# A decoder layer on one core: routing chain beside the shared expert, residual add split between ScalarE and GpSimd

## The chip, the cores and the metric

The kernel runs on one core of one Trainium2 chip, written in Bass, with every wait and semaphore by hand. The metric is the device time of one execution in microseconds (us), median of several. A core has TensorE (PE; its weight loads are shown as PEld), VectorE (DVE), ScalarE (ACT), GpSimd (POOL) and SyncE (SP, which here only starts DMAs). Each engine runs its own queue in order. All data are float32; "fp32r" is the rounded type that PE takes at one column a cycle.

## The reference

One pre-layernorm decoder layer over x of shape (8, 256, 512), that is 2048 tokens or 16 tiles of 128:

```
x = x + attn(layernorm(x))                        # linear attention, 16 heads
x = x + conv(ctx, ctx, layernorm(x), kernel, D)   # long convolution, 32 heads of 8 channels
x = x + ffn(layernorm(x))
ffn: scores = sigmoid(h @ gate_weight.T)          # 16 experts in 4 groups
     keep the 2 groups with the largest sum of their top 2, then the top 4 experts
     w = 2.5 * score / sum of the 4 scores
     out = sum_e w_e * (silu(h @ g_e.T) * (h @ u_e.T)) @ d_e.T      # I = 256
     shared = (silu(h @ sg.T) * (h @ su.T)) @ sd.T                  # every token
```

## The kernel before

It has five stages, each a block with its own SBUF; at a block's end the engines meet.

1. Attention, 0 to about 260 us, and the convolution, to 444. The convolution leaves its result, transposed (channels on partitions), in the tile `QY`.
2. The shared stage, lines 724 to 996, one step per tile of 128 tokens (16 of them). ScalarE copies the tile from `QY` to `ysl`; PE transposes it (`t3`); VectorE adds it from PSUM to `X` (`x2`, line 868) and takes mean and variance; GpSimd makes the reciprocal root (`rstd3`, 811 and 813); VectorE normalizes (`norm`, 878); PE transposes the result (`t4`); ScalarE and VectorE split it into a high part and a low part (`x_hi`, `x_lo`). PE then does gate and up of the shared expert (12 matmuls of 512 columns: a product of split operands takes three, lines 178 to 180), the router (8 of 32 columns), down of the tile before (6 of 512 columns) and a transpose of the hidden layer. VectorE adds the result to `X`, SP stores normalized rows to `xs_d` and `X` to `out`. The steps of neighbouring tiles are interleaved by hand.
3. The routing stage, lines 998 to 1284. VectorE alone runs some 110 dependent small operations over all 16 tiles: top groups, top 4, weights `W4`, counts per expert (two matmuls on PE), position of each token's row in a list sorted by expert and padded to slots of 512 (`DEST`). Then the list is inverted: for each tile VectorE makes one-hots (`colone`, `lowhot`), GpSimd and ScalarE make the products with token number and weight, and PE adds 4 matmuls a tile up into `PS[:, 2]` (`place`). From there come `IDX` (token of each row) and `WPOS` (its weight).
4. The slots, lines 1287 to 1535. 19 slots here, each of 512 rows of one expert. GpSimd gathers the rows by four indirect DMAs (`gathers`), PE transposes them, ScalarE and VectorE split them and the expert's weights, PE does gate and up with weights stationary (48 matmuls of 512 columns), and down of the slot before (24). ScalarE scales by `WPOS`, GpSimd adds to `out` by four indirect DMAs (`scatters`).

The order in each engine's queue is written out by hand in the `body` and `step` functions.

Of the kernel before, what the change touches and what calls it, by code (L numbers as in the profile page):

```python
# [16 lines left out]
P = 128  # L17
# [26 lines left out]
def decoder_program(nc, x, ctx2, qwT, kwT, vwT, owT, q_b, k_b, v_b, o_b, ssm, dskip, gateT, ebias,  # L44
                    gu_w, dn_w, c_ident, c_block, c_head, c_lt4, c_tri, c_free, c_slotk,
                    c_tok, out):
    with ExitStack() as ctx:
# [5 lines left out]


        kpad_d = nc.dram_tensor("kpad_d", (CH, KPAD + 1), F32).ap()
        xs_d = nc.dram_tensor("xs_d", (B * S + SLOT, D), F32).ap()
# [8 lines left out]
        Tz = [sb(f"Tz{k}", [P, D]) for k in range(2)]  # L65
        C2 = [sb(f"C2{k}", [P, DC * B, 2 * CD]) for k in range(2)]
# [7 lines left out]
        QY = sb("QY", [P, DC, B, S])  # L74
# [494 lines left out]
        zrow = sb("zrow", [P, D])  # L569
# [26 lines left out]
        with nc.Block() as block_:  # L596
            @block_.sync
            def _(sp):
# [5 lines left out]
                for t in range(SLOT_T):  # L604
                    rows = slice(B * S + t * P, B * S + (t + 1) * P)
                    sp.dma_start(xs_d[rows], zrow[:]).then_inc(zero_out, 16)
                    sp.dma_start(out[rows], zrow[:]).then_inc(zero_out, 16)
# [116 lines left out]
        x3h = [sb(f"x3h{p}", [P, DC, P], F32R) for p in range(2)]  # L724
        x3l = [sb(f"x3l{p}", [P, DC, P], F32R) for p in range(2)]
        sg = [sb(f"sg{p}", [P, I_FF]) for p in range(2)]
        hh = [sb(f"hh{p}", [P, I_FF]) for p in range(2)]
        hTh = [sb(f"hTh{p}", [P, IC, P], F32R) for p in range(2)]
        hTl = [sb(f"hTl{p}", [P, IC, P], F32R) for p in range(2)]
        LG = sb("LG", [P, NT, NE])  # L730
        table_row = sb("table_row", [P, 1])

# [6 lines left out]
        r_in = sem("r_in")  # L739
        st3 = ExitStack()  # L740

        def sb3(name, shape, dt=F32):
            return st3.enter_context(nc.sbuf_tensor(name, shape, dt))
        ysl = [sb3(f"ysl{p}", [P, DC, P]) for p in range(2)]
        xn3 = [sb3(f"xn3{p}", [P, D]) for p in range(2)]
        bst3 = [sb3(f"bn_stat3{p}", [P, 6]) for p in range(2)]
        mv3 = [sb3(f"mean_var3{p}", [P, 2]) for p in range(2)]
        ve3 = [sb3(f"var_eps3{p}", [P, 1]) for p in range(2)]
        rs3 = [sb3(f"rstd3{p}", [P, 1]) for p in range(2)]

        def pair(name):
            return [sem(f"{name}{p}") for p in range(2)]
        ysl_done, t3_ps, x2_done, bn3, mv3s, ve3s, rs3s, xn3_done = (
            pair(n) for n in ("ysl_done", "t3_ps", "x2_done", "ln2_bn", "ln2_mv", "ln2_ve", "ln2_rstd", "ln2_xn"))
        xs_out, t4_ps, x3_hi, x3_lo, rt_ps, lg_done, gu_ps, silu_done, h_done = (
            pair(n) for n in ("xs_out", "t4_ps", "x3_hi", "x3_lo", "rt_ps", "lg_done", "gu_ps", "silu_done", "h_done"))
        t5_ps, h_hi, h_lo, dn_ps, x3_done = (pair(n) for n in ("t5_ps", "h_hi", "h_lo", "dn_ps", "x3_done"))
        x3_out = sem("x3_out")


        def bank_chunks(bank, c=DC):
            return PS[:, bank, 0:c * P].rearrange("p (c n) -> p c n", c=c)

        def both_parts(bank):
            return PS[:, bank].rearrange("p (c n i) -> p c n i", c=IC, n=2)

        def gate_up(pe, p, done):
            for d in range(DC):
                mm = three_pass(pe, PS[:, 3 + p].rearrange("p (c n) -> p c n", c=IC), x3h[p][:, d], x3l[p][:, d],
                                gu_row(wh, d), gu_row(wl, d), d == 0, d == DC - 1)  # L770
            mm.then_inc(done, 1)

        def down(pe, p, done):
            for c in range(IC):
                mm = three_pass(pe, PS[:, 6 + p], hTh[p][:, c], hTl[p][:, c], wh[:, DC + c], wl[:, DC + c],
                                c == 0, c == IC - 1)
            mm.then_inc(done, 1)

        with nc.Block() as block_:
            @block_.sync  # L780
            def _(sp):

                sp.dma_start(eb[:], bass.AP(tensor=ebias.tensor, offset=0, ap=[[0, P], [1, NE]])).then_inc(r_in, 16)
                for dst, src in ((lt4, c_lt4), (tri, c_tri), (free, c_free), (slotk, c_slotk), (tok, c_tok)):
                    sp.dma_start(dst[:], src).then_inc(r_in, 16)

                def store_xn(i, p):
                    sp.wait_ge(xn3_done[p], i + 1)
                    sp.dma_start(xs_d[bass.ds((TPB * i + p) * P, P)], xn3[p][:]).then_inc(xs_out[p], 16)

                def store_x(i, p):

                    sp.wait_ge(x3_done[p], i + 1)
                    sp.dma_start(out[bass.ds((TPB * i + p) * P, P)], X[:, TPB * i + p]).then_inc(x3_out, 16)

                store_xn(0, 0)
                store_xn(0, 1)
                with sp.Fori(0, B - 1) as i:
                    for p in range(2):
                        store_xn(i + 1, p)  # L800
                        store_x(i, p)
                store_x(B - 1, 0)
                store_x(B - 1, 1)
                for p in range(2):
                    sp.wait_ge(xs_out[p], 16 * B)

            @block_.gpsimd
            def _(pool):
                def rstd3(i, p):
                    wait_apart(pool, mv3s[p], i + 1)  # L810
                    nc.gpsimd.tensor_scalar(ve3[p][:], mv3[p][:, 1:2], LN_EPS, None, ALU.add).then_inc(ve3s[p], 1)
                    pool.wait_ge(ve3s[p], i + 1)
                    nc.gpsimd.tensor_tensor(rs3[p][:], ve3[p][:], nhalf[:, 0:1], ALU.pow).then_inc(rs3s[p], 1)

                with pool.Fori(0, B) as i:
                    for p in range(2):
                        rstd3(i, p)

            @block_.scalar
            def _(act):  # L820
                def stage_y(i, p, first=False):

                    if not first:
                        wait_apart(act, t3_ps[p], i)
                    act.activation(ysl[p][:], QY[:, :, i, p * P:(p + 1) * P], ACT.Copy).then_inc(ysl_done[p], 1)

                def x_hi(i, p):
                    act.wait_ge(t4_ps[p], i + 1)
                    act.activation(x3h[p][:], bank_chunks(1), ACT.Copy).then_inc(x3_hi[p], 1)

                def silu(i, p):
                    act.wait_ge(gu_ps[p], i + 1)
                    act.activation(sg[p][:].rearrange("p (c n) -> p c n", c=IC), both_parts(3 + p)[:, :, 0], ACT.Silu
                                   ).then_inc(silu_done[p], 1)

                def hid_hi(i, p):
                    act.wait_ge(t5_ps[p], i + 1)
                    act.activation(hTh[p][:], bank_chunks(5, IC), ACT.Copy).then_inc(h_hi[p], 1)

                def step(i, p, last=False):  # L840

                    if not last or p == 0:
                        x_hi(i + p, 1 - p)
# [747 lines left out]
```

## Time and profile before

| | |
|---|---|
| median of 3 runs | 1023.42 us (1021.2 to 1024.94) |
| the profiled execution | 1022.06 us |
| its span, first to last instruction | 1020.2 us |
| mean granted clock of TensorE | 0.942 |
| busy: PE, DVE, ACT, POOL | 88%, 60%, 38%, 38% |

The span is one execution under the profiler. Stages can be told by their lines: 443.9 is the first copy of the shared stage (L825), 556 the sigmoid of the routing stage (L1084), 586.3 the first placement matmul (L1118), 621.9 the first step of the slots.

### The profile page before, as it was taken

Reading aid. Unit: us, or ns where it says so; the run is one execution under the profiler, and the core shown is the slowest. Engines: PE = TensorE matmul, PEld = TensorE weight load, DVE = VectorE, ACT = ScalarE, POOL = GpSimd, SP = SyncE. Lnnn points to the kernel's source line nnn. Section 1 sums busy time; section 2 is a strip of 40 time slices with the busy share of each in tenths; the row PEclk is TensorE's granted clock in tenths of the full one; section 3 lists DMA queues with packets and bytes.
Section 4 is the critical chain, followed back from the end, with each engine's and each line's share of the span. In section 5 each row is a group of like instructions: output and inputs, shape, how many; then the busy total and the mean of one; then the engine's idle time right before and its main releaser. Section 6 shows DMA issues by size and latency. Waiting matters only on the chain. (4 is left out here: it accounts for less than half of the span.)

```text
span 1020.2 us, 14917 instructions
## 1 busy us (share of the span) xinstructions
PE 897.3 (88%) x4428; PEld 739.2 (72%) x4428; DVE 614.0 (60%) x944; ACT 384.0 (38%) x658; POOL 391.8 (38%) x349
## 2 busy tenths in 40 slices
PE   4899999997779999949997095999999999999963
PEld 4788888885567777738885074778878878788752
DVE  5566666655269999966674993454454454454520
ACT  4322323331133343323232053455555555555521
POOL 3200000001156566711110053466666766766622
PEclk9999999998889999959999587999999999999987
DMA  8200000000333333202221011587887887878824
GB/s 318 95 1 1 0 0 0 0 1 0 132 125 104 108 109 110 74 27 74 82 82 72 0 63 62 168 185 203 196 197 194 193 207 194 183 202 205 184 43 60
DMA packets 47272, 108.54 MB, mean 106 GB/s; under 512 B 6736, under 2 KB 7248, under 8 KB 47120
## 3 DMA queue, kind: packets, MB, share of 16 engines
q0 software_dynamic: 17024, 39.86, 20.4%
q1 hardware_dynamic: 30224, 68.38, 20.3%
q8 instruction: 13, 0.21, 0.1%
q14 instruction: 11, 0.09, 0.0%
HBM read 77.73 MB, written 30.49 MB: 106 GB/s over the span
## 5 line engine op out<-in xcount | busy, mean ns | idle before, releaser
L189 PE MATMUL PS<-prod,Tz 128*128 128x288 f32 x640 | 161.7, 417 | 9.4 <-POOL prod L174 9.4
L1342 POOL DMA_INDIRECT out_y<-yo,idy x76 | 139.4, 1834 | 58.5 <-ACT yo L1386 46.3
L189 PEld LDWEIGHTS PS<-prod,Tz 128*128 128x128 f32 x640 | 125.1, 196 | 45.6 <-issue 6.0
L178 PE MATMUL PS<-xTh,wh 128*128 128x512 f32 x304 | 126.6, 416 | 7.7 <-issue 7.7
L180 PE MATMUL PS<-xTh,wl 128*128 128x512 f32 x304 | 120.4, 396 | 0.0
L179 PE MATMUL PS<-xTl,wh 128*128 128x512 f32 x304 | 120.0, 395 | 0.0
L1331 POOL DMA_INDIRECT xg<-xs_d,idx x76 | 86.5, 1138 | 35.4 <-issue 17.5
L1444 DVE TENSOR_TENSOR hTl<-hh,hTh 128x512 fp32r<-128x512 f32 x38 | 26.5, 697 | 111.9 <-ACT hTh L1380 107.7
L230 POOL TENSOR_SCALAR var_eps<-mean_var 128x2 f32<-128x2 f32 x16 | 3.5, 220 | 229.4 <-DVE mean_var L330 229.4
L171 POOL TENSOR_TENSOR prod<-C 128x1024 f32<-128x1024 f32 x32 | 61.3, 1917 | 66.3 <-PE PS L189 55.2
L178 PE MATMUL PS<-wh,hTh 128*128 128x512 f32 x184 | 74.6, 406 | 3.9 <-DVE hTl L1444 3.0
L1434 DVE TENSOR_TENSOR xTl<-PS,xTh 128x512 fp32r<-128x512 f32 x76 | 50.8, 688 | 44.6 <-ACT xTh L1372 44.6
L1429 DVE TENSOR_TENSOR wl<-ws,wh 128x1024 fp32r<-128x1024 f32 x57 | 68.3, 1224 | 11.7 <-ACT wh L1368 11.5
L1386 ACT ACTIVATE yo<-PS,WPOS 128x512 f32<-128x512 f32 x76 | 52.4, 690 | 59.0 <-PE PS L180 49.0
L179 PE MATMUL PS<-wl,hTh 128*128 128x512 f32 x184 | 72.9, 396 | 0.0
L180 PE MATMUL PS<-wh,hTl 128*128 128x512 f32 x184 | 72.8, 395 | 0.0
L699 DVE TENSOR_REDUCE QY<-term 128x2048 f32 (+1 forms) x32 | 72.7, 2270 | 0.1
L178 PEld LDWEIGHTS PS<-xTh,wh 128*128 128x128 f32 x304 | 58.1, 191 | 17.8 <-issue 8.2
L1372 ACT ACTIVATE xTh<-PS 128x512 fp32r<-128x512 f32 x76 | 44.5, 596 | 64.7 <-PE PS L1483 64.7
L180 PEld LDWEIGHTS PS<-xTh,wl 128*128 128x128 f32 x304 | 57.9, 190 | 12.8
L179 PEld LDWEIGHTS PS<-xTl,wh 128*128 128x128 f32 x304 | 58.3, 192 | 9.9
L1483 PE MATMUL PS<-ident,xg 128*128 128x128 f32 x304 | 48.1, 284 | 17.2 <-DMA xg<-xs_d,idx 11.2
(198 smaller groups left out, 1900.1 us busy)
## 6 DMA issues: line engine op xcount, KB each, us to landing
ws<-in_gu_w SPq DMA_DIRECT2D x38, 512.0 KB
ws<-in_dn_w SPq DMA_DIRECT2D x20, 512.0 KB, 5.2
C<-in_ctx SPq DMA_DIRECT2D x32, 256.0 KB, 2.6
Tz<-kpad_d SPq DMA_DIRECT2D x32, 256.0 KB, 3.1
xs_d<-xn SPq DMA_DIRECT2D x16, 256.0 KB, 2.1
out_y<-X SPq DMA_DIRECT2D x16, 256.0 KB, 2.0
X<-in_x SPq DMA_DIRECT2D x1, 3072.0 KB, 18.9
xg<-xs_d,idx POOLq DMA_INDIRECT x76
```

The costliest lines, as they stand in the source:

```text
L171: nc.gpsimd.tensor_tensor(o[:, :, 0:4 * CD].rearrange("p a (s j) -> p a s j", s=4), a[:, :, 0:CD].unsqueeze(2).broadcast_to([P, LB, 4, CD] ...
L178: pe.matmul(out_, lh, rh, start=first, stop=False)
L179: pe.matmul(out_, lh, rl, start=False, stop=False)
L180: return pe.matmul(out_, ll, rh, start=False, stop=last)
L189: mm = pe.matmul(PS[:, DC * k + c].rearrange("p (b n) -> p b n", n=YGAP)[:, :, 0:NPAIR], Tz[k][:, (c - m) * P:(c - m + 1) * P], prod[k][:, ...
L699: dve.tensor_reduce(QYh[:, :, bass.ds((2 * i + k) * CD, CD)], term[k][:].rearrange("p s a j u -> p a j s u"), AX_XY, ALU.add).then_inc(red ...
L1331: nc.gpsimd.indirect_dma_start(out=xg[:, t], out_offset=None, in_=xs_d, in_offset=bass.IndirectOffsetOnAxis(ap=idx[:, t:t + 1], axis=0)).t ...
L1342: nc.gpsimd.indirect_dma_start(out=out, out_offset=bass.IndirectOffsetOnAxis(ap=idy[:, t:t + 1], axis=0), in_=yo[:, t], in_offset=None, co ...
L1386: act.activation(yo[:, t], PS[:, 6 + t % 2], ACT.Copy, scale=WPOS[:, bass.ds(SLOT_T * s + t, 1)]).then_inc(yo_done, 1)
L1429: dve.tensor_tensor(expert_part(wl, part), expert_part(ws, part), expert_part(wh, part).bitcast(F32), ALU.subtract).then_inc(w_lo5, 1)
L1434: dve.tensor_tensor(xTl5[:, d], PS[:, 4 + d % 2], xTh5[:, d].bitcast(F32), ALU.subtract).then_inc(xT_lo5, 1)
L1483: mm = pe.transpose(PS[:, 4 + d % 2, t * P:(t + 1) * P], xg[:, t, d * P:(d + 1) * P], ident[:])
```

## The change

Stages 2, 3 and 4 become one block, and the order within it is new.

- All 16 tiles are first brought through residual, layernorm, transposes and router, without the shared expert. PE transposes straight from `QY`; ScalarE copies the result from PSUM to SBUF (`y_copy`), GpSimd adds it to `X` (`x2`), VectorE keeps the statistics and `x3_lo`, ScalarE normalizes by Identity with scale and bias (`norm`), for which GpSimd makes a third small number (`nb3`).
- The shared expert then runs like a slot, on groups of 512 tokens with weights stationary. Its hidden layer is made by GpSimd from two ScalarE copies (`up`, `hidden`, `hid_lo`), its output kept in SBUF (`y_shared`) and added to `X` by VectorE only during slot 0.
- VectorE's routing chain runs beside the shared expert's matmuls, and the placement matmuls stand between them. The weight isn't placed any more: it is stored as 16 more columns of each row of `xs_d` (528 instead of 512 floats) and comes with the gather; GpSimd takes the expert's column out (`weights`). Only one product (`colhot`) is left, made by VectorE in the rounded type.
- The sum over the four choices for `SEL` is two adds instead of a reduction; `W4` becomes `WE`, of shape [P, NT, NE].
- GpSimd waits for all stores of `X` once, before its `body(1)`.

```diff
-        xs_d = nc.dram_tensor("xs_d", (B * S + SLOT, D), F32).ap()
+        xs_d = nc.dram_tensor("xs_d", (B * S + SLOT, D + NE), F32).ap()
...
             @block_.sync
...
+                for i in range(NT):
+                    sp.wait_ge(xn3_done, i + 1)
+                    sp.dma_start(xs_d[i * P:(i + 1) * P, 0:D], xn3[i % NX]).then_inc(xs_out[i % NX], 16)
+                sp.wait_ge(we_done, 1)
+                sp.dma_start(xs_d[0:B * S].rearrange("(t p) n -> p t n", p=P)[:, :, D:], WE[:]).then_inc(we_out, 16)
...
+                sp.wait_ge(es_done, 2)
                 e = expert_of(sp, 0)
                 for part in range(NPART):
-                    load_part(sp, e, part)
-
+                    load_part(e, part)
+                last = last_slot(sp)
+                next_slot(0)
+                for i in range(NT):
+                    sp.wait_ge(x3_done, i + 1)
+                    sp.dma_start(out[i * P:(i + 1) * P], X[:, i]).then_inc(x3_out, 16)
+                with sp.Fori(1, NFULL - 1) as s:
+                    next_slot(s)
...
+            @block_.gpsimd
+            def _(pool):
+                def x2(i):
+                    wait_apart(pool, y_copied, i + 1)
+                    nc.gpsimd.tensor_tensor(X[:, i], X[:, i], sg5[i % 2][:], ALU.add).then_inc(x2_done, 1)
+
+                def rstd3(i):
...
+                    wait_apart(pool, rs3s, i + 1)
+                    nc.gpsimd.tensor_scalar(nb3[k][:], mv3[k][:, 0:1], rs3[k][:], -1.0, ALU.mult, ALU.mult).then_inc(nb3s, 1)
+
+                def hidden(g, c):
+                    wait_apart(pool, up5, IC * g + c + 1)
+                    nc.gpsimd.tensor_tensor(hh5[c][:], hh5[c][:], sg5[c][:], ALU.mult).then_inc(hh_done5, 1)
+
+                def hid_lo(g, c):
+                    wait_apart(pool, h_hi5, IC * g + c + 1)
+                    nc.gpsimd.tensor_tensor(hTl5[:, c], hh5[c][:], hTh5[:, c].bitcast(F32), ALU.subtract).then_inc(h_lo5, 1)
...
+                def weights(s):
+                    wait_apart(pool, xg_in, 16 * SLOT_T * (s + 1))
+                    e = expert_of(pool, s)
+                    nc.gpsimd.tensor_copy(WPOS[:, bass.ds(SLOT_T * s, SLOT_T)].unsqueeze(2), xg[:, :, bass.ds(e + D, 1)]
+                                          ).then_inc(wpos_done, 1)
...
+                def body(s):
+                    weights(s)
+                    gathers(s + 1)
+                    scatters(s - 1, first=isinstance(s, int) and s == 1)
+
+                nc.gpsimd.memset(ones[:], 1.0).then_inc(memsets, 1)
+                x2(0)
+                for i in range(NT):
+                    if i + 1 < NT:
+                        x2(i + 1)
+                    rstd3(i)
+                for g in range(NG - 1):
+                    for c in range(IC):
+                        hidden(g, c)
+                        hid_lo(g, c)
+                hidden(NG - 1, 0)
+                wait_apart(pool, idx_ready, 1)
+                all_rows_out(pool)
+                wait_apart(pool, we_out, 16)
...
+                gathers(0, first=True)
+                hid_lo(NG - 1, 0)
+                hidden(NG - 1, 1)
+                hid_lo(NG - 1, 1)
+                last = last_slot(pool)
+                weights(0)
+                gathers(1)
+                wait_apart(pool, x3_out, 16 * NT)
+                body(1)
...
             @block_.scalar
             def _(act):
+                def y_copy(i):
+                    if i >= 2:
+                        wait_apart(act, x2_done, i - 1)
+                    act.wait_ge(t3_ps, i + 1)
+                    act.activation(sg5[i % 2][:], PS[:, 4 + i % 2], ACT.Copy).then_inc(y_copied, 1)
+
+                def norm(i):
...
+                    wait_apart(act, nb3s, i + 1)
+                    act.activation(xn3[i % NX], X[:, i], ACT.Identity, scale=rs3[k][:], bias=nb3[k][:]).then_inc(xn3_done, 1)
...
+                act.activation(table_row[:], ident[:, 0:1], ACT.Sigmoid)
+                y_copy(0)
+                for i in range(NT):
+                    if i + 1 < NT:
+                        y_copy(i + 1)
+                    norm(i)
+                    if i > 0:
+                        x3_hi(i - 1)
+                x3_hi(NT - 1)
+                act.wait_ge(lg_done, 1)
                 act.activation(SC[:], LG[:], ACT.Sigmoid).then_inc(score_done, 1)
...
             @block_.tensor
             def _(pe):
...
+                t3(0)
+                t3(1)
+                for i in range(NT):
+                    t4(i)
+                    if i + 2 < NT:
+                        t3(i + 2)
+                    if i > 0:
+                        router(i - 1)
+                router(NT - 1)
+
+                shared_gate_up(0, 0)
+                shared_gate_up(0, 1)
+                shared_gate_up(1, 0)
                 pe.wait_ge(sel_done, 1)
...
+                pe.matmul(PS[:, 4, 0:NT * NE], tri[:], sel, start=True, stop=True)
+                pe.matmul(PS[:, 4, NT * NE:], ones[:], sel, start=True, stop=True).then_inc(count_ps, 1)
+                shared_down(0)
+                shared_gate_up(1, 1)
+                shared_gate_up(2, 0, placing=0)
+                shared_down(1, placing=SLOT_T)
+                shared_gate_up(2, 1, placing=2 * SLOT_T)
+                shared_gate_up(3, 0, placing=3 * SLOT_T)
+                shared_down(2)
+                shared_gate_up(3, 1)
+                pe.wait_ge(idx_ready, 1)
+                for d in range(DC):
+                    x_transposed(0, d)
+                pe.wait_ge(es_done, 2)
+                last = last_slot(pe)
+                body(0)
+                body(1)
...
             @block_.vector
             def _(dve):
+                def stats(i):
...
+                for i in range(NT):
+                    stats(i)
+                    if i >= 2:
+                        x3_lo(i - 2)
...
+                def one_hots(t):
+                    p = t % HOT
+                    if t >= HOT:
                         wait_apart(dve, hot_used, t - HOT + 1)
...
+                    dve.tensor_tensor(lowhot[p], free[:].unsqueeze(1).broadcast_to([P, TOPK, P]),
+                                      LOW[:, t].unsqueeze(2).broadcast_to([P, TOPK, P]), ALU.is_equal).then_inc(low_hot, 1)
+                    for r in range(TOPK):
+                        dve.tensor_scalar(colhot[p][:, r], free[:, 0:NCOL], HIF[:, t, r:r + 1], TOKV[:, t, r:r + 1],
+                                          ALU.is_equal, ALU.mult).then_inc(col_hot, 1)
...
+                w_lo(0, 1)
+                add_shared(0)
+                hidden(0, 0)
+                add_shared(1)
+                add_shared(2)
+                hid_lo(0, 0)
+                w_lo(0, 2)
+                w_lo(1, 0)
+                for d in range(DC):
+                    x_lo(1, d)
+                add_shared(3)
                 body(1)
```

In the text, (g, c) is the half c of gate and up of group g of the shared expert; slot 0 (0, 1) is the second half of slot 0, between whose pieces the transposes of slot 1 stand.

## Rows read from the trace of the kernel before

**Rows 1.** The page, part 1: busy us, share of the span, instructions.
```profile
PE 897.3 (88%) x4428; PEld 739.2 (72%) x4428; DVE 614.0 (60%) x944; ACT 384.0 (38%) x658; POOL 391.8 (38%) x349
```
**Rows 2.** Windows: stretch, length, busy of each engine, granted clock, DMA share, GB/s.
```profile
443.90:555.20 111.30, 103.78 (x576) 88.14 (x576) 68.59 (x144) 31.78 (x66) 12.54 (x32) 0.93 0.20 75
555.20:586.30 31.10, 2.07 (x4) 1.18 (x5) 26.79 (x113) 4.45 (x8) 1.50 (x2) 0.54 0.02 9
586.30:621.40 35.10, 32.90 (x128) 25.33 (x128) 31.43 (x37) 19.01 (x60) 16.77 (x15) 0.92 0.13 46
670.30:971.40 301.10, 294.90 (x1411) 240.12 (x1409) 143.52 (x177) 161.98 (x241) 198.46 (x160) 1.00 0.83 196
0.00:25.00 25.00, 11.72 (x67) 10.94 (x68) 13.79 (x15) 11.02 (x11) 7.20 (x12) 1.00 0.89 316
```
**Rows 3.** Timeline of PE, shared stage's start: start, length, engine, line, form, idle before.
```profile
452.97 1.11 PE L947 MATMUL PS<-ident,xn 128*128 128x128 f32 x4 [2.42 <-DVE xn L878]
453.88 1.06 PE L940 MATMUL PS<-ident,ysl 128*128 128x128 f32 x4
```
**Rows 4.** Timeline of PE in the middle of the shared stage.
```profile
522.38 0.60 PE L947 MATMUL PS<-ident,xn 128*128 128x128 f32 x4
...
522.81 0.60 PE L940 MATMUL PS<-ident,ysl 128*128 128x128 f32 x4
...
523.49 0.39 PE L179 MATMUL PS<-wl,x3h 128*128 128x512 f32 x1
...
523.72 0.40 PE L180 MATMUL PS<-wh,x3l 128*128 128x512 f32 x1
```
**Rows 5.** Windows late in attention: transposes alone, then the first wide matmuls.
```profile
249.00:251.00 2.00, 1.14 (x7) 1.14 (x7) 0.05 (x1) 0.60 (x1) 0.00 (x0) 0.50 0.00 0
...
253.00:257.00 4.00, 3.67 (x9) 2.92 (x10) 0.19 (x1) 0.00 (x0) 0.00 (x0) 0.50 0.00 0
```
**Rows 6.** Groups by line and form: count, busy, mean ns of one, idle before.
```profile
L1386 ACT ACTIVATE yo<-PS,WPOS 128x512 f32<-128x512 f32 x76 | 52.4, 690 | 59.0 <-PE PS L180 49.0 <-issue 9.3 <-DMA out_y<-yo,idy 0.7
...
L1138 POOL TENSOR_TENSOR QY<-QY,TOKV 128x496 f32<-128x496 f32 x16 | 18.1, 1129 | 44.2 <-DVE QY L1264 44.2
...
L829 ACT ACTIVATE x3h<-PS 128x512 fp32r<-128x512 f32 x16 | 9.6, 598 | 7.4 <-PE PS L947 6.7
```
**Rows 7.** Timelines of GpSimd and VectorE around the first reciprocal root of the shared stage.
```profile
447.80 0.23 POOL L811 TENSOR_SCALAR var_eps<-mean_var 128x1 f32<-128x1 f32 x1 [12.33 <-DVE mean_var L872]
448.12 0.57 POOL L813 TENSOR_TENSOR rstd<-var_eps,nhalf 128x1 f32<-128x1 f32 x1
...
448.83 0.55 DVE L878 TENSOR_SCALAR xn<-X,mean_var,rstd 128x512 f32<-128x512 f32 x1 [1.22 <-POOL rstd L813]
```
**Rows 8.** Timelines of VectorE and PE in the routing stage, in order of time.
```profile
557.97 0.43 DVE L1163 TENSOR_TENSOR BI<-SC,eb 128x256 f32<-128x256 f32 x1 [2.73 <-ACT SC L1084]
...
570.74 1.22 PE L1109 MATMUL PS<-SEL,tri 128*128 128x256 f32 x2 [16.23 <-DVE SEL L1212]
...
574.35 0.42 DVE L1223 COPY TOT<-PS 128x256 f32<-128x256 f32 x1
...
584.07 0.68 DVE L1264 TENSOR_TENSOR QY<-free,HIF 128x496 f32<-128x496 f32 x1
...
585.27 1.49 DVE L1264 TENSOR_TENSOR QY<-free,HIF 128x496 f32<-128x496 f32 x1
```
**Rows 9.** Timelines of GpSimd and PE at the start of the slots.
```profile
621.89 0.19 POOL L1328 COPY idx<-IDX 128x4 uint32<-128x4 uint32 x1 [3.31 <-POOLq L1070]
...
631.47 1.97 PE L1483 MATMUL PS<-ident,xg 128*128 128x128 f32 x8 [10.75 <-DMA xg<-xs_d,idx]
...
635.83 0.76 PE L178 MATMUL PS<-xTh,wh 128*128 128x512 f32 x1
```
**Rows 10.** Timelines of PE and GpSimd: start of slot 2, and an index copy in slot 2.
```profile
670.31 0.48 PE L178 MATMUL PS<-xTh,wh 128*128 128x512 f32 x1
...
689.67 0.19 POOL L1328 COPY idx<-IDX 128x4 uint32 x1 [3.24 <-PE PS L1483]
```

More of the change, by code:

```diff
@@ L773, in down @@
[L773 to L777, printed above, removed]
+        ones = sb("ones", [P, P])
+        LG = sb("LG", [P, NT, NE])
+        SC = sb("SC", [P, NT, NE])
+        BI = sb("BI", [P, NT, NE])
+        MB = sb("MB", [P, NT, NE])
+        g_hi, g_lo = sb("g_hi", [P, NT * 4, 2]), sb("g_lo", [P, NT * 4, 2])
@@ new lines, in next_parts, with body @@
+                def next_parts(s, final=False):
+                    hid_hi(s + NG, 0)
+                    w_hi(s, 2)
+                    if not final:
+                        w_hi(s + 1, 0)
+                        for d in range(DC):
+                            x_hi(s + 1, d)
+                def body(s, final=False):
+                    second = isinstance(s, int) and s == 1
+                    silu(s - 1 + NG, 1)
+                    hid_hi(s - 1 + NG, 1)
+                    w_hi(s, 1)
+                    silu(s + NG, 0)
+                    for t in range(SLOT_T):
+                        y_out(s - 1, t, second)
+                    next_parts(s, final)
@@ new lines, in _ @@
+                for d in range(DC):
+                    x_hi(0, d)
+                hid_hi(NG - 1, 1)
+                act.wait_ge(es_done, 2)
+                last = last_slot(act)
+                w_hi(0, 1)
+                silu(NG, 0)
+                for t in range(SLOT_T):
+                    y_shared_out(NG - 1, t)
+                next_parts(0)
+                body(1)
+                with act.Fori(2, NFULL - 1) as s:
+                    body(s)
+                with act.Fori(NFULL - 1, NSLOT - 1) as s:
+                    with act.If(s < last):
+                        body(s)
@@ new lines, in shared_down, with x_transposed @@
+                def shared_down(g, placing=None):
+                    for t in range(SLOT_T):
+                        down5(g, t, first=(g == 0))
+                        if placing is not None:
+                            place(placing + t)
+                def x_transposed(s, d):
+                    if d == 0:
+                        pe.wait_ge(xg_in, 16 * SLOT_T * (s + 1))
+                    if not (isinstance(s, int) and s == 0 and d < 2):
+                        pe.wait_ge(xT_lo5, DC * s + d - 1)
+                    for t in range(SLOT_T):
+                        mm = pe.transpose(PS[:, 4 + d % 2, t * P:(t + 1) * P], xg[:, t, d * P:(d + 1) * P], ident[:])
+                    mm.then_inc(xT_ps5, 1)
```

881 lines of the change are left out of this document (332 added, 549 removed).

## The prediction

> **What bounds the kernel now.** I read the page first: TensorE is busy for 897 of 1020 us [rows 1], so the only time to win lies where it idles or runs slowly. The windows by stage say where [rows 2]. In the slot loop (670.3 to 971.4) PE is busy 295 of 301 us at full clock. In the shared stage (443.9 to 555.2) it is busy 104 of 111 us: 16 tiles, one after the other, through four engines. In the routing stage it does almost nothing for 31 us (555.2 to 586.3, 2.1 us busy) while VectorE's chain of small steps runs, then 35 us of placement matmuls, which come one tile per 2 us. The first gather and transposes follow; the first slot matmul starts at 635.83 [rows 9]. So 443.9 to 670.3, where slot 2 begins [rows 10], is 226.4 us, and that is all that the change rebuilds; what lies before and the slots behind keep their order of work.
>
> **The change, part by part.** The new stage has two halves. A: for all 16 tiles residual, layernorm, transposes, router. B: the shared expert in groups of 512 tokens, with the routing chain beside it.
>
> *Half A: one dependence sets its pace.* PE's order is t4(i), t3(i+2), router(i-1). t4(i) waits for norm(i). t3(i+2), though its data is there, stands behind t4(i). ScalarE's y_copy(i+2) needs t3(i+2); GpSimd's x2(i+2) needs y_copy(i+2); and GpSimd's rstd3(i+1) stands behind x2(i+2) in its own queue, and norm(i+1) waits for it. That is a ring through three engines, one turn a tile:
> - norm on ScalarE, a 128x512 with pointer scale: 0.70 (0.69 for such a form, 0.60 plain) [rows 6];
> - two sets of four transposes. At half clock 452.97 to 454.94, 1.97 [rows 3]; at full clock 522.38 to 523.41, 1.03 [rows 4];
> - y_copy 0.60 [rows 6];
> - x2, a 128x512 add on GpSimd. The nearest row is its 128x496 product, 1.13 mean [rows 6]; I take 1.10, bounds 1.0 and 1.3;
> - rstd3: 0.23, then 0.57 starting 0.32 later [rows 7], and one more small operation, 0.3 with its gap: 1.27;
> - handing over: GpSimd to VectorE cost 0.14 [rows 7]; four such hops, two of them almost free: 0.42.
> Sum 6.06 at half clock, 5.1 at full clock. Which clock? PE starts this half at 1.2 GHz (the transposes of rows 3 ran there), and in the old trace it was at 1.2 GHz in a stretch (249 to 251) in which it had nothing but such transposes, and still when wide matmuls followed [rows 5]. Half A holds only transposes and 32-column router matmuls, so I take 1.2 GHz throughout. The first norm ends at 450.9 (1.28 of table load, t3, y_copy, x2, x2 again, then stats, rstd3 and norm behind the start at 443.9). Fourteen turns are 84.8; from norm(14) to the last router matmul are 5.4 (second rstd3, norm, 1.1 transposes, 0.6 and 0.7 for the split, 1.5 router). Half A ends at T = 541.1: 97 us for work that used to share its tiles with the expert's matmuls. That is the cost: the old stage took 111 with them.
>
> *Half B.* A 512-column matmul starts every 0.23 us at full clock [rows 4], so a half of gate/up (24) is 5.46 and a down (24) also 5.46. The first 4 us run at half clock, as at 253 to 257 [rows 5], which loses 2.0. In us behind T: gate/up (0,0), (0,1), (1,0) end at 18.4. VectorE's way to SEL was 12.7 from BI (557.97 to the release of PE at 570.7) [rows 8]; with logits and sigmoid ahead it ends near 13.5: hidden. The two count matmuls: 1.2 at full clock. VectorE then needs 9.7 from TOT to the first one-hot (574.35 to 584.07) [rows 8] and 1.3 for this; PE meanwhile does down(0) and (1,1), to 30.5, and one piece of (2,0): hidden to within a microsecond. Sixteen places of four matmuls follow between pieces of 1.37. A 124-column matmul in the rounded type is in no row; four transposes start within 0.43 [rows 4], so 0.11 below, and the old one cost 0.26 per pass (32.9 over 128) [rows 2], which is the upper end. I take 0.15 (the 32-column and 128-column kinds are nearer): 9.6. Stalls for late one-hots: the SLE steps put 3.1 us between the second and third, 0.8 is left over. So (2,0) to (3,0) take 32.2 without contention.
>
> *A cost of its own: the two engines on SBUF.* VectorE's one-hot product took 0.68 us at 584.07, with GpSimd idle, and 1.49 at 585.27, beside a GpSimd product [rows 8]. In half B GpSimd has 16 operations of 1.1 us for the hidden layer, all beside the chain or the one-hots; about two fall into the 11 us in which the chain has no slack. I take 1.5 us, bounds 0 and 6. The Trainium skill has the rule behind this (GPSIMD Engine Reference, section 1, Specifications): GpSimd's SBUF interfaces are shared with VectorE, and a VectorE instruction with two SBUF inputs contends. Rows 8 agree. By the rule half A pays nothing, as its VectorE operations have at most one SBUF input; without any contention the sum would be 1.5 better.
>
> *Into the slots.* PE is through (3,0) at 64.2, down(2) and (3,1) at 75.1. GpSimd must do hidden(3,0), ready at 66.1, before the first gather; with waits 66.4. From index copy to first transpose were 9.6 (621.89 to 631.47), to the first matmul 4.4 more [rows 9]: slot 0 starts at 80.4. Of the 14 us from index copy to first matmul [rows 9], 5.3 stay visible. Slot 0 (0,0), perhaps at half clock again (5.3 us of transposes and waiting precede it; I take 1 of 2 us), down(3), (0,1) with the next transposes (7.2): to 99.4.
> Then a new wait. GpSimd waits for all 16 stores of X before scatters, and this wait stands ahead of gathers(2). SP issues the stores behind the third weight part of slot 1, free at about 96. Behind it queue 4.5 MB. At 316 GB/s, the rate of the first 25 us [rows 2], they take 14; at 196, the slot loop's rate, 23. I take 13.5, near the first since nothing else moves then: 109.5. The gather adds 0.9 (expert number, copy) and 9.2: 119.6. PE wants it at 112.4, so it stalls 7.2. The rest of slot 1 is 5.7: slot 2 starts at T + 125.3.
> *Slots.* Per slot GpSimd gets one small copy and a register load, some 0.8 us; it waited 3.24 us for PE there [rows 10]. Nothing, at the upper end 0.2 a slot (3 us) for rows of 2112 instead of 2048 bytes.
>
> **Sum.** 541.1 + 125.3 - 670.3 = -3.9 us. The profiled execution took 1022.06, which gives 1018.2; it lay 1.4 under the median of the runs, 1023.42, so 1019.5 is predicted for the median.
>
> **The rivals.**
> *The clock rises in half A.* For it speaks that PE works in every turn, where rows 3 come after 10 us of idling; against it rows 5. A turn is then 5.1, T 13 us earlier, and 3 us of cold starts are gone: 1004.
> *The stores decide; slower.* If stores and weights drain at the slot loop's 196 GB/s, they land at 119 instead of 109.5, and slot 2 begins 9.5 later: 1029. The change is slower than before once they land after T + 113.4, that is 17.4 us for 4.5 MB or below 259 GB/s. For it: 196 is what the loop moves in steady state; against it: 316 was reached with rows of the same 2 KB, and the loop's is slowed by read-modify-write scatters.
> *GpSimd and VectorE block each other more widely*, at every hidden and hid_lo: 16 times 0.8 on the chain and one-hots, at most 6 us of it visible instead of 1.5: 1024. The chain has little slack, but one-hots have 0.6 us a tile.
> *The ring does not close* (it does not do what I say): if t3 and y_copy ran ahead, ScalarE with three 128x512 operations and GpSimd with 2.4 us a tile would set 2.6 a tile, and the time would be near 970. The order of the queues speaks against it.
>
> **How the numbers follow.** My forecast 0.55, its own range 1012 to 1027 (turn 5.8 to 6.4, for x2 at 1.0 to 1.3; places 0.11 to 0.26; stores 12 to 17 us); clock 0.2; stores slower 0.12; wide blocking 0.1; no ring 0.03. The range of 8 in 10 is 1001 to 1030; it leaves out most of the last case and the ends of the others. A measurement tells about 0.5% from no change, 1018.3 to 1028.5. Faster: 0.2 + 0.03 + 0.55 x 0.42 = 0.46. Slower: 0.08 of the stores' 0.12, 0.03 of the blocking, 0.06 of the forecast's tail: 0.17. Same: 0.37.
>
> **What would show it.** A turn of half A: t4 follows t4 by 6.06 us, y_copy waits for t3's transposes, GpSimd's x2 for y_copy, granted clock 0.50 from 444 to 541. The logits' reduction at 541. PE above 95% busy behind T for 75 us, no wait for SEL. One-hots on VectorE 1.3 a tile, longer where GpSimd works. GpSimd's first gather 66 us behind T; its wait for stores ending 110 behind T, PE idle 7 us ahead of the transposes of slot 2. Slots at 18.72. I am wrong if a turn is under 5.5 or over 6.6, or if slot 2 starts elsewhere than 120 to 130 behind T.

## The result: slower by 1.5%

The changed kernel takes 1038.05 us (median of 4 runs, 1036.63 to 1038.75) against 1022.31 (4 runs, 1021.1 to 1024.94) on the same chip: ratio 1.0149, 95% interval 1.0124 to 1.0174. Predicted were 1019.5, range 1001 to 1030. The profiled execution has a span of 1036.9 us, 16.7 more than before, where the prediction's sum had 3.9 less. So 20.6 us are to be found.

Page of the changed kernel, part 1, to be read against [rows 1]: TensorE's work is the same, its share fell from 88% to 87%; it waits more.

```profile
PE 899.1 (87%) x4332; PEld 743.7 (72%) x4332; DVE 581.5 (56%) x911; ACT 385.1 (37%) x616; POOL 412.0 (40%) x401
```

Windows by stage, columns as in [rows 2]: half A, half B, from there to the start of slot 2, the slots.

```profile
443.90:549.20 105.30, 56.02 (x256) 53.44 (x255) 25.10 (x48) 31.27 (x50) 36.85 (x64) 0.50 0.11 42
549.20:624.30 75.10, 72.02 (x333) 58.03 (x332) 61.11 (x196) 21.51 (x36) 26.15 (x19) 0.98 0.13 38
624.30:683.10 58.80, 44.01 (x192) 34.93 (x192) 28.55 (x39) 22.14 (x34) 20.31 (x20) 0.85 0.65 189
684.00:990.00 306.00, 297.56 (x1406) 239.45 (x1404) 142.50 (x177) 161.57 (x241) 187.98 (x176) 1.00 0.83 192
```

Half A lasts 105.3 us at 1.2 GHz, and no engine is busy for more than 53% of it: that is what a ring looks like. Half B is as full as forecast (72.0 of 75.1). Between its end and slot 2 TensorE idles for 15 us.

One turn of half A, timelines of ScalarE, TensorE, GpSimd and VectorE in order of time:

```profile
456.15 0.81 ACT L990 ACTIVATE xn<-X,shift,rstd 128x512 f32<-128x512 f32 x1 [3.01 <-POOL shift L899]
457.02 1.12 PE L1108 MATMUL PS<-ident,xn 128*128 128x128 f32 x4 [4.51 <-ACT xn L990]
457.93 1.06 PE L1099 MATMUL PS<-ident,QY 128*128 128x128 f32 x4
459.02 0.60 ACT L982 ACTIVATE sg<-PS 128x512 f32<-128x512 f32 x1 [1.57 <-PE PS L1099]
459.80 1.26 POOL L890 TENSOR_TENSOR X<-X,sg 128x512 f32<-128x512 f32 x1 [3.77 <-ACT sg L982]
461.15 0.22 POOL L895 TENSOR_SCALAR var_eps<-mean_var 128x1 f32<-128x1 f32 x1
...
462.21 0.27 POOL L899 TENSOR_SCALAR shift<-mean_var,rstd 128x1 f32<-128x1 f32 x1 [0.21 <-POOL rstd L897]
462.61 0.81 ACT L990 ACTIVATE xn<-X,shift,rstd 128x512 f32<-128x512 f32 x1 [2.99 <-POOL shift L899]
```

Each line waits for the one above it or follows it in its engine's queue, and the last is the first, one tile on, 6.46 us later. All fourteen turns (transposes at 450.54 and again at 541.88) average 6.52.

The ends of the halves, timelines of VectorE, TensorE and GpSimd:

```profile
549.27 0.69 DVE L1282 TENSOR_REDUCE LG<-PS 128x256 f32<-128x512 f32 x1 [1.98 <-PE PS L1117]
567.37 0.59 PE L1210 MATMUL PS<-SEL,tri 128*128 128x256 f32 x2
615.46 0.19 POOL L913 COPY idx<-IDX 128x4 uint32<-128x4 uint32 x1
624.03 0.39 PE L185 MATMUL PS<-QY_rounded,wl 128*128 128x512 f32 x1
631.12 0.76 PE L183 MATMUL PS<-y_rounded,wh 128*128 128x512 f32 x1
```

And what answers to [rows 9, 10] at slot 2, timelines of SP, GpSimd and TensorE:

```profile
648.17 11.23 SPq L878 DMA_DIRECT2D out_y<-X  x16
663.11 0.18 POOL L923 COPY WPOS<-xg 128x4 f32 x1 [21.13 <-DMA out_y<-X]
663.47 0.19 POOL L913 COPY idx<-IDX 128x4 uint32<-128x4 uint32 x1 [0.17 <-POOL WPOS L923]
...
675.70 1.11 PE L1170 MATMUL PS<-ident,xg 128*128 128x128 f32 x4 [10.81 <-DMA xg<-xs_d,idx]
...
683.15 0.48 PE L183 MATMUL PS<-y_rounded,wh 128*128 128x512 f32 x1
```

GpSimd sits 21 us in its wait for the 16 stores, then gathers, and TensorE waits 10.8 us for that gather. 683.15 is the matmul that stood at 670.31 in [rows 10]: 12.84 later. Of the 16.7 us by which the span grew, the other 3.9 lie in the slots. Index copies thirteen slots apart, to be read against 689.67 [rows 10] and the line of the kernel before that ends this fence:

```profile
702.64 0.19 POOL L913 COPY idx<-IDX 128x4 uint32 x1 [2.98 <-PE PS L1170]
...
948.77 0.19 POOL L913 COPY idx<-IDX 128x4 uint32 x1 [2.98 <-PE PS L1170]
```
```profile
933.15 0.19 POOL L1328 COPY idx<-IDX 128x4 uint32 x1 [2.21 <-PE PS L1483]
```

That is 18.93 us a slot; before (689.67 to 933.15) it was 18.73.

### The profile page after: what moved, and what is told of

It is laid out like the page before. It is cut to its first block, busy times and chain, and to the rows that moved or that the text cites. A ratio compares the mean times of both kernels' runs of the same rounds, so it can differ in the third digit from the quotient of the medians.

```text
span 1036.9 us, 14426 instructions
## 1 busy us (share of the span) xinstructions
PE 899.1 (87%) x4332; PEld 743.7 (72%) x4332; DVE 581.5 (56%) x911; ACT 385.1 (37%) x616; POOL 412.0 (40%) x401
## 4 chain that ended last, share of the span: by engine, by line
PE 31%; issue 7%; DVE 6%; ACT 5%; POOL 5%; DMA 2%; ACTq 0%; SPq 0%; POOLq 0%; DVEq 0%
PE PS L183 9%; PE PS L185 8%; PE PS L184 8%; PE PS L1170 2%; POOL X L890 2%; DVE C_rounded L1378 2%; PE PS L1108 2%; ACT wh L1015 2%; DVE y_rounded L1402 1%; DMA xg<-xs_d,idx 1%; ACT xn L990 1%; PE PS L1099 1%; ACT hTh L1007 1%; DVE wl L1397 1%; ACT sg L982 1%
## 5 line engine op out<-in xcount | busy, mean ns | idle before, releaser
L183 PE MATMUL PS<-y_rounded,wh 128*128 128x512 f32 x336 | 142.0, 423 | 7.7 <-issue 7.7
L933 POOL DMA_INDIRECT out_y<-QY,idy x76 | 124.3, 1636 | 61.3 <-ACT QY L1026 44.2
L185 PE MATMUL PS<-y_rounded,wl 128*128 128x512 f32 x336 | 134.4, 400 | 0.0
L184 PE MATMUL PS<-y_rounded,wh 128*128 128x512 f32 x336 | 134.3, 400 | 0.0
L1411 DVE TENSOR_TENSOR hTl<-hh,hTh 128x512 fp32r<-128x512 f32 x38 | 26.3, 693 | 114.3 <-ACT hTh L1007 114.3
L1402 DVE TENSOR_TENSOR y_rounded<-PS,y_rounded 128x512 fp32r<-128x512 f32 x76 | 50.9, 688 | 54.6 <-ACT y_rounded L1019 54.5
L183 PEld LDWEIGHTS PS<-y_rounded,wh 128*128 128x128 f32 x336 | 65.1, 194 | 19.6 <-issue 8.1
L185 PEld LDWEIGHTS PS<-y_rounded,wl 128*128 128x128 f32 x336 | 64.9, 193 | 15.5
L1026 ACT ACTIVATE QY<-PS,WPOS 128x512 f32<-128x512 f32 x76 | 52.3, 689 | 61.0 <-PE PS L185 61.0
L184 PEld LDWEIGHTS PS<-y_rounded,wh 128*128 128x128 f32 x336 | 65.3, 194 | 11.5
L1019 ACT ACTIVATE y_rounded<-PS 128x512 fp32r<-128x512 f32 x76 | 44.9, 595 | 69.4 <-PE PS L1170 69.4
```

Of the source, the lines that this page charges most:

```text
L183: pe.matmul(out_, lh, rh, start=first, stop=False)
L184: pe.matmul(out_, lh, rl, start=False, stop=False)
L185: return pe.matmul(out_, ll, rh, start=False, stop=last)
L933: nc.gpsimd.indirect_dma_start(out=out, out_offset=bass.IndirectOffsetOnAxis(ap=idy[:, t:t + 1], axis=0), in_=yo[:, t], in_offset=None, co ...
L1026: act.activation(yo[:, t], PS[:, 6 + t % 2], ACT.Copy, scale=WPOS[:, bass.ds(SLOT_T * s + t, 1)]).then_inc(yo_done, 1)
L1402: dve.tensor_tensor(xTl5[:, d], PS[:, 4 + d % 2], xTh5[:, d].bitcast(F32), ALU.subtract).then_inc(xT_lo5, 1)
```

## The experiments

Ratios are to the kernel before, from runs on the same chip; "after" is the changed kernel, 1.0149. Unless said, each starts from it.

**1. Which queue closes the ring.** TensorE's order:

```
-  t4(i);  t3(i+2);  router(i-1)
+  t3(i+2);  t4(i);  router(i-1)
```


> Change: in half A TensorE's order is t3(i+2), t4(i), router(i-1) instead of t4(i), t3(i+2), router(i-1). Theory (the ring through TensorE and GpSimd sets half A): the eight transposes leave the ring. A ring stays, as ScalarE's y_copy(i+2) stands behind norm(i), norm(i) behind rstd3(i), and this behind x2(i+1) and y_copy(i+1): y_copy 0.60, x2 1.26, rstd3 1.36, norm 0.81, x3_hi 0.60, hops 0.3, so a turn of 4.9 us instead of 6.5. Fourteen turns give 22 us: half A ends near 527, the run near 1016. Rival 1 (TensorE at 1.2 GHz is too slow for half A, whatever the order): the turn stays 6.5 and the run near 1038. Rival 2 (the GpSimd queue alone sets the turn): 1.26 + 1.36 = 2.6 a turn, the run near 985.

1012.89 us, ratio 0.9892 (0.9875 to 0.9908). A turn is 4.85 us (transposes of xn at 488.04 and 492.89), VectorE's reduction of the logits moves from 549.27 to 524.52. The expectation had 4.9, so the ring theory holds to 0.05 us a turn.

**2. The add back on VectorE.**

```
-  ScalarE: y_copy(i): sg5 <- PSUM        GpSimd: x2(i): X += sg5
+  VectorE: x2(i): X += PSUM
```


> Change: the residual x2 is added by VectorE straight from PSUM; ScalarE's y_copy and GpSimd's x2 are gone, the rest is as in the changed kernel (TensorE still has t4(i) ahead of t3(i+2)). Theory (the ring is closed only through y_copy and x2 on the way to rstd3): nothing that norm(i+1) needs stands behind t3(i+2), the ring opens, and TensorE's own work sets the turn: 1.97 of transposes and 1.7 of router at 1.2 GHz, 3.7 us, 14 x 2.8 = 39 us less, half A ends near 510, the run near 999 (below 990 if the clock rises once TensorE is busy all the time). Rival (the turn is what hand-overs norm, transposes, x3_hi, x3_lo cost, and x2 has little to do with it): only the 0.6 and 1.26 are replaced by 0.7, turn 5.3, the run near 1021.

991.71 us, 0.9688 (0.9662 to 0.9714). The turn is 3.33 us, below my 3.7: eight transposes and eight router matmuls end to end. So this one part of the change costs 46 us, and what is left of it would have won 31. The granted clock stayed at 0.50, which leads to experiment 6.

**3. Or only its place in GpSimd's queue.** GpSimd and ScalarE keep their parts:

```
-  x2(i+1);  rstd3(i)
+  rstd3(i);  x2(i+1)
```


> Change: the changed kernel with two lines of GpSimd's queue swapped: rstd3(i) stands ahead of x2(i+1) instead of behind it. GpSimd still adds, ScalarE still copies. Theory (the add costs by its place in the queue, not by its length): norm(i+1) no longer waits for the add of the tile after it. What is left of the ring is norm 0.72, eight transposes 1.97 and y_copy 0.60, ahead of norm(i+1) on ScalarE, with hops 3.5 to 3.8 a turn; beside it y_copy, x2, stats, rstd3, norm is 3.7 a turn. A turn of 3.8 instead of 6.5, 14 x 2.7 = 38 us: half A ends near 511 and the run takes near 1000. Rival (what costs is that the add is on the slow engine, two more hand-overs and 1.26 a tile): a turn of 5 or more, the run at 1015 or above.

1005.16 us, 0.9832 (0.9804 to 0.9859): 33 us for two lines swapped. GpSimd's timeline shows what sets the turn of 3.92 now:

```profile
487.33 1.27 POOL L890 TENSOR_TENSOR X<-X,sg 128x512 f32<-128x512 f32 x1
489.96 0.22 POOL L895 TENSOR_SCALAR var_eps<-mean_var 128x1 f32<-128x1 f32 x1 [1.36 <-DVE mean_var L1245]
...
491.25 1.27 POOL L890 TENSOR_TENSOR X<-X,sg 128x512 f32<-128x512 f32 x1
```

A smaller ring: add 1.27, wait for VectorE's statistics 1.36, the three steps of rstd3 1.29. The expectation had 3.8 from another ring (norm, eight transposes, y_copy); that one does not bind, since ScalarE still waits 0.46 us a turn for rstd3 before norm, so the near hit in the number is partly luck. So of the 46 us the order in one queue is 33; the slower engine and the detour are 13.

**4. The wait for the stores.**

```
-  wait(x3_out);  weights(1);  gathers(2);  scatters(0)
+  weights(1);  gathers(2);  wait(x3_out);  scatters(0)
```


> Change: GpSimd's wait for the 16 stores of X stands behind gathers(2), ahead of the first scatter, instead of ahead of gathers(2). Theory (the wait holds the gather back, and TensorE waits 10.8 us for it): the gather starts near 650 instead of 663.5, is there when TensorE wants it; the next late thing is the first scatter, 7 us earlier than now, and y_out(1) behind it, worth 1 to 3 us. Slot 2 starts 8 to 10 us earlier, the run takes 1028 to 1030. Rival (the DMA queues full of stores and weights are the limit, not the wait): the gathers land only when the stores have drained, slot 2 starts at most 3 us earlier, the run takes 1035 to 1038.

1030.0 us, 1.0053 (1.0036 to 1.007): 10 us less by the ratios, 8 by the medians. The index copy of gathers(2) moves from 663.47 to 652.54, and TensorE no longer waits for that gather at all, where it waited 10.8 us. What comes last ahead of slot 2 is now a wait of 3.0 for split rows:

```profile
672.03 0.66 PE L1171 MATMUL PS<-ident,xg 128*128 128x128 f32 x4 [3.03 <-DVE y_rounded L1403]
```

In ScalarE's queue these rows stand behind the conversion of the next gate/up weights, which starts at 669.06 after 2.9 us of waiting for their load; SP had issued this load at 663.24, behind the 16 stores, which it took 12.6 us to issue. (The 2.4 us that TensorE waits for a gather in this trace are slot 0's, at 627.70; they were 2.9 in the changed kernel. The expectation of experiment 5 takes them for the moved gather's, and the 3.0 for y_out's; neither is so.) The wait in GpSimd's queue, not the load of the DMA queues, held the gather.

With the add on VectorE as well:


> Change: the add on VectorE (as in the run before, 991.7) and GpSimd's wait for the stores behind gathers(2). Theory (two separate costs, one in half A, one ahead of slot 2): the 8.05 us that the moved wait gave alone come off again, 983 to 985. Rival (with half A shorter something else is late at slot 2 as well): less than 4 us, 988 or above.

983.42 us, 0.9618 (0.959 to 0.9646), 0.7% under experiment 2: the two costs add up, within the intervals.

**5. Earlier, larger stores.** On top of that:

```
   SP: load gate/up halves of slot 1
+  SP: store groups 0, 1, 2 (1 MB each)
   SP: load down weights of slot 1
-  SP: 16 stores of 256 KB
+  SP: store group 3
```


> Change: the add on VectorE, the later wait, and on the SP queue X stored in four DMAs of 1 MB, three of them ahead of the load of slot 1's down weights (the adds of their groups are over 3 to 10 us before it) instead of 16 of 256 KB behind it. Theory (after the wait has moved, TensorE still waits 2.4 us for the gather and 3.0 for y_out behind the first scatter, and both wait for the stores to drain): the stores end 6 to 10 us earlier and most of the 5.4 us go, 978 to 981. Rival (4 MB take as long whenever they start, as weights and gathers share the queues): within 1.5 us of the kernel without this step. Slower would be the case where the gather of slot 1 now shares the queues with the stores.

983.27 us, 0.9618 (0.96 to 0.9636): nothing. The waits of TensorE between 500 and 680 (what it waited for: us in all, times, longest), first without, then with this step:

```profile
PE PS L1155 <- DMA xg<-xs_d,idx: 4.2, 2, 2.6
...
PE PS L1155 <- DVE y_rounded L1392: 2.9, 3, 2.0
```
```profile
PE PS L1161 <- DMA xg<-xs_d,idx: 7.0, 3, 3.7
...
PE PS L1161 <- DVE y_rounded L1398: 1.6, 3, 1.0
```

The waits for the split rows shrank by 1.3: ahead of slot 2 ScalarE no longer waits for its weights, as it did for 1.8 us. The waits for gathers grew by 2.8: slot 1's, which now runs beside the stores, from 1.6 to 3.7, and slot 2's from nothing to 1.0. That is the case named last in the expectation. The balance can't be drawn to a microsecond, as the profiled execution with this step took 987.62 us, 4.4 above the median, and the one without it 984.75.

**6. The clock.** Four extra matmuls of 128x512 in each turn, whose result nobody reads, first in the changed kernel:

```
   router(i-1)
+  4 x matmul(PS[0 or 1], wh, wh)
```


> Change: four extra 128x512 matmuls in each turn of half A (behind router(i-1), into two PSUM banks that nobody reads then), where TensorE idles 3 us a turn; nothing else. Theory (of the 6.5 us of a turn 1 us is the price of the 1.2 GHz clock on the eight transposes, the rest is latency of the other engines): if the extra work brings the clock to 2.4 GHz, a turn is 5.5, the router's and the first 3 us of half B at full clock come on top, half A ends 15 us earlier and the run takes 1020 to 1024. Rival (the clock stays at 1.2 GHz with TensorE 75% busy, too): the turn stays at 6.5, or 7 where the extra 1.7 us lie in the way of t4; the run takes 1038 to 1045.

1041.62 us, 1.0173 (1.0156 to 1.019): the turn stays 6.54, the clock too. Then with the add on VectorE:


> Change: the add on VectorE, and four extra 128x512 matmuls in each turn of half A whose result nobody reads. There TensorE was at 1.2 GHz although it worked 97 to 99% of the time with 128- and 32-column operations. Theory (the narrow operations leave the clock low, wide ones bring it up): at 2.4 GHz a turn is 1.03 of transposes, 0.9 of router and 0.92 of the extra ones, 2.85 instead of 3.33, and half B begins warm: the run takes 982 to 987. Rival (the clock stays at 1.2 GHz all through this half): 1.7 us a turn more, 14 x 1.7 = 24 us, the run near 1015.

986.72 us, 0.9653 (0.9635 to 0.9672), where 0.9688 was without; the intervals touch, but from the first transpose to the reduction of the logits half A went from 59.8 us to 54.8. Windows in the middle of half A: the changed kernel, it with the extra matmuls, the add on VectorE, this with the extra matmuls:

```profile
480.00:510.00 30.00, 14.76 (x69) 14.31 (x69) 7.47 (x15) 8.86 (x14) 10.85 (x20) 0.50 0.09 35
```
```profile
480.00:510.00 30.00, 24.18 (x88) 19.61 (x89) 7.49 (x15) 8.87 (x14) 10.82 (x20) 0.50 0.09 36
```
```profile
480.00:510.00 30.00, 29.77 (x128) 27.82 (x128) 17.49 (x39) 11.08 (x17) 6.26 (x18) 0.50 0.16 62
```
```profile
480.00:500.00 20.00, 19.20 (x128) 16.25 (x128) 12.83 (x24) 9.12 (x15) 5.22 (x15) 1.00 0.21 80
```

TensorE 99% busy with transposes and 32-column matmuls ran at 1.2 GHz; 81% busy with wide ones among them, and a wait in every turn, still 1.2; 96% busy with wide ones, 2.4 GHz. At 2.4 a turn is 2.9 us although it holds more work. So the rival "the clock rises" did not come true: with the ring's wait in every turn the clock stayed low even beside wide matmuls.

**7. The slots.** Wider rows in the kernel before:

```
-  xs_d rows of 512, xg[.., 512]
+  xs_d rows of 528, xg[.., 528]   (16 more numbers, zeros, stored once at the start)
```


> Change: the kernel before, with rows of 528 instead of 512 numbers in the gather's source and in the gathered tile (the 16 more are zeros), nothing else. Theory A (the wider rows slow the slots, by more bytes in odd-sized packets beside TensorE's reads): the period of a slot goes from 18.72 to 18.9 us, the run from 1022 to 1026. Theory B (it is where tiles lie in SBUF, or another part of the change): period 18.72, run unchanged.

1028.62 us, 1.0053 (1.0039 to 1.0068). Index copies eleven slots apart:

```profile
732.60 0.19 POOL L1329 COPY idx<-IDX 128x4 uint32 x1 [3.25 <-PE PS L1484]
...
940.83 0.19 POOL L1329 COPY idx<-IDX 128x4 uint32 x1 [3.35 <-PE PS L1484]
```

18.93 a slot. To exclude the place of the tiles, the hidden tiles hTh5 and hTl5 of the changed kernel were moved:


> Change: the changed kernel with the tiles of the split hidden layer placed ahead of the shared expert's tiles in SBUF instead of behind the gathered rows (the others move up by 8 KB); nothing else. Theory B (placement): the down matmuls go back to 0.227 us and the period of a slot below 18.8, the run to 1034 or 1035. Theory A (wider rows): period 18.93, the run at 1038.

1039.27 us, 1.0157 (1.0142 to 1.0171), 18.93. And in the kernel before an unused 256 bytes stood behind the gathered rows, which were left narrow:


> Change: the kernel before with an unused tile of 256 bytes per partition behind the gathered rows, which moves all later tiles as far as the wider rows did; the rows stay 2048 bytes. Theory A (the wider rows slow the slots): slot period 18.72 us, down matmuls every 0.227, the run at 1023 like the kernel before. Theory B (the address of the tiles): 18.92, 0.233 and 1028.

1022.86 us, 1.0 (0.999 to 1.0009), 12 slots apart:

```profile
727.30 0.19 POOL L1329 COPY idx<-IDX 128x4 uint32 x1 [2.11 <-PE PS L1484]
...
952.08 0.19 POOL L1329 COPY idx<-IDX 128x4 uint32 x1 [3.36 <-PE PS L1484]
```

18.73. So it is the width of the rows, 0.2 us a slot. Of the 5.5 us that it cost the kernel before, the slots are 3.7. Part of the other 1.8 seems to lie in the shared stage, which stores into the wider rows: from its first copy (L825) to the sigmoid it lasts 114.3 us in the trace with wide rows, 113.5 and 113.2 in the two with narrow ones.

**8. What all of it gives.** The add on VectorE, the later wait, the extra matmuls:


> Change: the add on VectorE, GpSimd's wait for the stores behind gathers(2), and four extra 128x512 matmuls a turn in half A (result unread). Theory (three separate costs): 983.4 less the 5 to 7 us that the clock gave alone, 976 to 979. Rival (the time won in half A is lost again at slot 2, where stores and gathers are late): 982 or above.

978.67 us, 0.9565 (0.9544 to 0.9586). Then four of the turns with work of half B in place of the extra matmuls (which in the other turns now write to one PSUM bank instead of two):


> Change: as e12_warm_best, but in four of the turns the extra matmuls are replaced by the shared expert's first gate/up half (24 matmuls of 128x512, in PSUM banks free then), which leaves half B. Theory (half B is set by TensorE up to the count matmuls, then by VectorE's one-hots): the count matmuls run when SEL is there, 2 to 3 us earlier, and the rest of half B follows; the turns with six instead of four wide matmuls cost 0.5 us each: net 1 to 3 us less than e12_warm_best. Rival (half B is bound by TensorE all through): the whole 5.5 us less 2. Rival 2 (the one-hots alone bind): no difference.

981.49 us, 0.9589 (0.9565 to 0.9614), not better; the 1 to 3 us expected did not come. The count matmuls now waited 3.0 us for SEL, and IDX came 64.1 us behind the logits' reduction as against 63.9, though TensorE had 24 matmuls less to do there. VectorE was busy for 59.6 of these 64 us (59.7 before): it is its chain as a whole that binds half B. Half A itself lasted 58.6 us instead of 57.3. Last, ten extra matmuls ahead of the first layernorm, on top of 978.67:

```
   t3(0);  t3(1)
+  10 x matmul(PS[0 or 1], wh, wh)
```


> Change: as e12_warm_best (978.7), and ten more 128x512 matmuls between t3(1) and t4(0), where TensorE waits 3.6 us for the first layernorm. Theory (the first turns still run at 1.2 GHz because TensorE came out of idleness): the clock is up by the second or third turn instead of the fourth, 1.5 to 3 us less, 976 to 977. Rival (ten at 1.2 GHz last 4.3 us, longer than the wait, and t4(0) comes 0.7 later for nothing): 979 to 980.

975.27 us, 0.9527 (0.9507 to 0.9547): 4.7% faster than the kernel before and the best version; its step over 978.67 is at the edge of the intervals. Half A starts at another time in each profiled execution (first transpose between 442.8 and 446.3), so its length has to be compared, and not where it ends: from there to the logits' reduction it took 51.9 us, as against 57.3 in the run that it builds on and 54.8 in experiment 6, where half A has the same code. The two differ by when the clock rose, at 465 and at 458; with the ten matmuls in front it rose at 451. So half A gave 2.9 to 5.4 us, against 1.5 to 3 expected, and the median 3.4.

## Why the prediction was wrong

The mechanisms were right: the ring closed as described, the clock was 0.50 throughout half A, and GpSimd's wait for the stores held up slot 2. Terms of the sum in three places were sized too low, all to one side, and they add to the 20.6 us. By the prediction's own signs a turn of 6.52 was still allowed (5.5 to 6.6), but the start of slot 2, 133.95 behind T, was not (120 to 130).

- **Half A, 8.1 us.** T was 541.1 in the forecast and 549.2 on the chip. A turn was 6.52 on average instead of 6.06; in the one shown (6.46) norm took 0.81 for 0.70, x2 1.26 for 1.10, rstd3 1.33 for 1.27, the hand-overs 0.49 for 0.42. Fourteen times 0.46 is 6.5 us. The tail was 7.3 instead of 5.4: t4(15) had to wait in TensorE's queue for router(13) (543.09 to 544.8), and router(14) stood ahead of router(15), which the forecast left out. The first norm was 0.4 early, as the block began at 443.45 instead of 443.9. The 0.70 came from a ScalarE row with a scale only [rows 6]; with a bias tile beside it the same shape takes 0.81. (The Trainium skill, ScalarE: Activation LUTs, section What ACT_TABLE_LOAD costs, gives about 93 ns for each pointer operand; 0.60, 0.69 and 0.81 agree, and by it norm would have been 0.80.) The 1.10 was chosen under a row of 1.13 for fewer elements, from a range up to 1.3: the wrong end. In a ring such a tenth counts fourteen times.
- **From T to slot 2, 8.65 us** (133.95 instead of 125.3). Half B's end itself was right to 0.3 us: gate/up ended at T + 18.2 (18.4), the index copy came at T + 66.3 (66.4), (3,1) ended at T + 75.1 (75.1). Slot 0 began at T + 81.9 (80.4), 15.7 us behind the index copy instead of 14.0. Then the step "16 stores": they started at T + 99.0 (96) and landed at T + 113.9 (109.5). The rival "the stores decide" had T + 113.4 as its turning point and 0.12 as its chance: the point was passed by half a microsecond, but not through the slow drain that the rival names. From 648 to 663 the DMA engines moved 329 GB/s, more than the 316 I took; the stores started 3 us later and took 14.9 us instead of 13.5, of which SP spent 11.2 in issuing them. The gather behind them took 12.6 us to the first transpose, not 10.1, and the rest of slot 1 7.45, not 5.7: behind its wait of 10.8 us TensorE ran at a granted clock of 0.50 until 678 and was back at 1.00 by 680.
- **The slots, 3.9 us.** "Nothing, at the upper end 0.2 a slot" was the wrong end again; experiment 7 measured 0.2, and that the rows' width does it. For the 17 slots from slot 2 on that is 3.4; the last half microsecond is not traced.

The forecast's own range (1012 to 1027) was too narrow because its terms were summed at their middle or low ends; most landed near their high end or past it. Half A's 8.1 us alone would have turned the forecast gain of 3.9 into a loss. The chance of slower, 0.17, was taken mostly from the rivals and not from the terms of the sum. The ring's own worth the prediction had about right: its rival without a ring stands near 970, some 50 us lower, and experiment 2 gives 46.

The contention term was right in kind and a little low. VectorE's SEL, a 128x256 with two inputs, took 1.42 us beside GpSimd's product where SM, of the same form right behind it, took 0.43; four one-hot steps took 1.10 alone and 2.08 beside GpSimd's product, which itself went from 1.29 to 1.96:

```profile
579.87 1.10 DVE L1378 TENSOR_SCALAR C_rounded<-free,HIF,TOKV 128x124 fp32r<-128x124 f32 x4
...
581.49 2.08 DVE L1378 TENSOR_SCALAR C_rounded<-free,HIF,TOKV 128x124 fp32r<-128x124 f32 x4
```
```profile
568.83 1.29 POOL L903 TENSOR_TENSOR hh<-hh,sg 128x512 f32<-128x512 f32 x1 [2.06 <-ACT hh L1003]
...
580.76 1.96 POOL L903 TENSOR_TENSOR hh<-hh,sg 128x512 f32<-128x512 f32 x1 [3.13 <-ACT hh L1003]
```

At SEL it stayed hidden: SEL was there 2.5 us before TensorE asked for it. At the one-hots it did not: 5 of the 16 took 2.1 us instead of 1.1, and TensorE waited for one-hots four times, 3.0 us in all, where the forecast had 0.8 of stalls and 1.5 of contention. The one-hot steps read one tile and two pointer operands, so here the slowdown was not limited to VectorE instructions with two tiles as inputs. That half B came out to 0.3 us all the same is in part luck.

## What to carry to other kernels

Where several engines hand a tile on, write down each queue's order and look for a ring: an operation of the next tile ahead of one that this tile still needs. Its turn is the sum of latencies, no engine looks busy, and swapping two lines can be worth more than moving work between engines. Put a wait directly ahead of the instruction that needs it, not ahead of a gather that does not. And a stage of short operations can pay for TensorE's lower clock too: look at its granted clock. Here, once the ring was open, four wide matmuls a turn beside the short ones went with 2.4 GHz and cost less than they saved; with the ring closed they changed nothing.

## What the runs showed of the hardware

- Width of gathered rows and TensorE: with rows of 2112 bytes the matmuls of the down projection start every 0.2331 us, with 2048 every 0.2267 (ten slots each, experiment 7's kernels), at nearly the same DMA rate (194 and 196 GB/s) and full clock; the gate/up ones hardly change (0.238 and 0.237). The Trainium skill (SBUF — State Buffer, section Who interferes with whom) says that a DMA never contends with a compute engine. If the gathers' transfers are what slows the matmuls, this case is against that rule: 18.93 us a slot instead of 18.73. Shown is that wider rows do it and moved tiles do not; that it goes through the DMA, and on which path, no run here shows.
- TensorE's clock: in experiment 2 the 54 us from 451 to 505, with narrow operations alone and one wait of 0.8 us, were run at 1.2 GHz; with wide ones among them it was at 2.4 GHz from 459 on (experiment 6) and from 465 on (experiment 8, the same code there).
- GpSimd's 128x512 add with two inputs in SBUF takes 1.26 us; its product and subtraction of the same form take 1.26 to 1.30, and up to 2.34 beside VectorE. ScalarE's 128x512 with scale and bias tiles takes 0.81, with a scale 0.69, plain 0.60.
